# Probabilities as the stationary operand in the product with the context, in a fused gated cross-attention and expert block

## The chip, the cores and the metric

The program runs on one core of a Trainium2 chip. The time is device time in microseconds for one execution, and the figure that counts is the median of the runs. A core has a matrix engine (PE; its weight loads are shown apart, as PEld), a vector engine (DVE), an activation engine (ACT), a general engine (POOL) and a queue that issues transfers (SP). Each works through its own instructions in order; they meet at semaphores. A matmul holds one operand in the array (stationary, loaded by a LDWEIGHTS) and streams the other past it (moving); its result goes to PSUM, which has 8 banks of 512 fp32 columns.

## The reference

There are 16 batches, each with 100 query tokens of width 128 and a context of 1444 rows of width 96; cross-attention has 16 heads of width 64. What matters here, cut down:

```python
q = heads(layernorm(x) @ w_q);  k = heads(context @ w_k);  v = heads(context @ w_v)
attn = softmax(q @ k.T / 8, axis=-1)            # per head: 100 x 1444
x = x + tanh(g_xattn) * (merge(attn @ v) @ w_o + b_o)
# then self-attention over the 100 tokens (16 heads of width 8),
# a router over 8 experts (two picked), the experts and a shared expert
x = x + tanh(g_ffn) * ffn(layernorm(x))
```

## The kernel before

The weights of keys and queries are folded into one matrix per head (`Mh`), those of values and output into another (`Nh`). So the kernel never makes keys or values: scores are the context times `qk` (96 x 1600, the 16 heads' 100 queries side by side), and the product of probabilities and values is (probabilities times context) times `Nh`.

The cross-attention of one batch goes in 24 steps, numbered 0 to 23. The first twelve belong to heads 0 to 7 (half 0, 800 query columns), the others to heads 8 to 15 (half 1). Within a half each step takes one chunk of up to 128 context rows (the twelfth has 36). In step i PE first computes the scores of chunk i (`score_unit`, six matmuls of 400 columns, in fp16 parts hi*hi, hi*lo and lo*hi). ACT takes two exponentials of them (`probs`), one fp32 into `p32` and one fp16 into `p_hi`. DVE, or POOL in the even steps from 6 to 20, subtracts the two into `p_lo` (`probs_rest`). PE then multiplies the probabilities of step i-2 with the context (`pv_unit`, L747): stationary is the chunk of context (`c_hi` or `c_lo`, 128 x 128, whose column 96 is all ones so that the sum of the probabilities comes along), moving are 400 columns of probabilities, six matmuls in all. The result, context dimension by query, gathers in two PSUM banks (`ACCB`) over twelve steps. ACT copies it to `acc_sb` (`acc_evac`, at steps 13 and 1) and the next half starts in the same banks.

Everything else of a batch is cut into small units, which a plan (`plan`) places into the 24 steps: `t` and `q` transpose the next batch's context and make its `qk`; 39 `p` units compute a bound for the scores of the next batch, each one matmul of 512 or 420 columns (L813) whose row maximum DVE takes (L1247); `y` units multiply `acc_sb` with `Nh` (L840), three heads to a unit with the sum in a 129th column, DVE divides by that sum (L1265, L1269) and POOL adds the heads one by one onto `x1` (`add_heads`, L566); `ln`, `xf` and `f0` to `f13` are the self-attention; `rs` and `h2` the norm before the router. Half 1 of a batch is finished in the next batch (`y1`), half 0 in its own (`y0`).

The units that use PE share two PSUM banks in turn (`AUXB`). A unit waits until the unit two before it in this order has been read out of its bank. DVE does that reading for nearly all units; for `f6` to `f9` ACT does it (`by_act`, L999), and ACT does it after the two exponentials of its step. Within a step PE works in this order: scores, the first third of the step's units, the two hi*hi matmuls of the product with the context, the second third, the other four matmuls, the last third. A list of n units is cut at n//3 and 2n//3. The other engines keep the same order of units. The plan's `p` units go where the plan's own figures for DVE's load (`LOAD`) leave room, in steps 3 to 20.

In steps 1 to 6 this gives, with the thirds parted by a bar: step 1 `t2 | q0 | q1`; step 2 `q2 | q3 | y1,0`; step 3 `y1,1 | p0 | p1`; step 4 `y1,2 | p2 | p3`; step 5 `p4 | p5 | p6`; step 6 `ln | p7 | p8`. Then step 8 `xf | f0 | p13`; step 9 ` | f1 | p14`; step 10 ` | f2 | p15`; step 14 `f8 | p21 | p22 p23`; step 15 `y0,0 | f9 p24 | p25 p26`; step 16 `y0,1 | f10 | p27`.

After the last batch a list (`LAST`) mixes the remaining units of that batch with the first pieces of the experts; the rest of the experts follows.

## Time and profile before

| | us |
|---|---|
| median of 3 runs (lowest, highest) | 1574.19 (1571.65, 1574.80) |
| span of the profiled execution | 1570.3 |
| median over that span | 3.9 |
| sixth batch (batch 5), steps 0 to 23, from 490.6 to 571.9 | 81.3 |
| start of batch 0 / of batch 15 / end of batch 15's steps | 70.2 / 1328.4 / 1405.0 |

The profiled execution's own time isn't listed apart from its span; the 3.9 us between the span and the median of the runs stand for what lies around it. In a row of the timeline the columns are the start in us from the span's start, the time from the first start to the last end, the engine, the line, the operation with its tiles and shapes (partitions x elements; before a matmul's shape stands rows*columns of the stationary operand), and xcount, how many were merged. A matmul's shown duration holds the time to drain the array, so matmuls that follow each other overlap in it, and their pace is the distance of their starts. An fp32 matmul has two records.

### The profile page before, as it was taken

How to read it: one execution, taken by the hardware profiler on the slowest of the kernel's cores; microseconds unless marked ns; L12 is line 12 of the kernel's file. 1: busy time of each engine (PE TensorE's matmuls, PEld its weight loads, DVE VectorE, ACT ScalarE, POOL GpSimd, SP SyncE). 2: the span in 40 equal slices, each digit the busy share in tenths (PEclk: the TensorE clock that was granted, in tenths of full speed). 3: DMA queues.
4: the chain of work that ended last, by engine and by line, in shares of the span. 5: the costliest groups of instructions: out<-in, count | busy, mean ns of one | idle time of the engine just before them, and what ended most of it. 6: DMA issues, size and time to landing. Idle time of an engine off the chain costs nothing.

```text
span 1570.3 us, 29033 instructions
## 1 busy us (share of the span) xinstructions
PE 1432.2 (91%) x8968; PEld 849.7 (54%) x8968; DVE 1085.7 (69%) x1948; ACT 832.3 (53%) x1236; POOL 561.2 (36%) x705
## 2 busy tenths in 40 slices
...
DMA packets 14994, 18.08 MB, mean 12 GB/s; under 512 B 3046, under 2 KB 12490, under 8 KB 14858
## 3 DMA queue, kind: packets, MB, share of 16 engines
...
## 4 chain that ended last, share of the span: by engine, by line
PE 59%; DVE 17%; issue 9%; ACT 6%; POOL 5%; DMA 1%; DVEq 1%; POOLq 0%; ACTq 0%; SPq 0%
PE psum L747 13%; PE psum L728 7%; PE psum L813 6%; PE psum L732 6%; PE psum L730 6%; DVE mx L1247 4%; PE psum L840 4%; PE psum L760 3%; PE psum L862 3%; ACT p_hi L952 3%; PE psum L853 3%; PE psum L773 2%; DVE p_lo L431 2%; DVE kbd L1276 2%; POOL p_lo L431 2%
## 5 line engine op out<-in xcount | busy, mean ns | idle before, releaser
L951 ACT ACTIVATE p<-psum 128x800 f32<-128x800 f32 (+1 forms) x384 | 321.3, 837 | 564.1 <-PE psum L732 558.2
L1247 DVE TENSOR_REDUCE mx<-psum 128x1 f32<-128x512 f32 (+3 forms) x624 | 387.2, 652 | 63.5 <-PE psum L813 58.5
L431 POOL TENSOR_TENSOR p_lo<-p,p_hi 128x800 f16<-128x800 f32 x128 | 236.3, 1847 | 472.9 <-ACT p_hi L952 461.2
L952 ACT ACTIVATE p_hi<-psum 128x800 f16<-128x800 f32 (+1 forms) x384 | 318.8, 830 | 0.0
L431 DVE TENSOR_TENSOR p_lo<-p,p_hi 128x800 f16<-128x800 f32 (+1 forms) x256 | 269.2, 1051 | 54.5 <-ACT p_hi L952 25.5
L813 PE MATMUL psum<-cT_hi,qk_hi 96*128 96x512 f16 (+3 forms) x624 | 236.2, 389 | 47.2 <-DVE mx L1247 15.0
L747 PE MATMUL psum<-p_hi,c_hi 128*128 128x400 f16 (+1 forms) x768 | 197.4, 338 | 21.3 <-POOL p_lo L431 14.7
L728 PE MATMUL psum<-qk_hi,cT_hi 97*128 97x400 f16 (+1 forms) x768 | 198.3, 340 | 11.7 <-ACT p_hi L952 5.5
L730 PE MATMUL psum<-qk_lo,cT_hi 96*128 96x400 f16 (+1 forms) x768 | 198.0, 339 | 0.0
L732 PE MATMUL psum<-qk_hi,cT_lo 96*128 96x400 f16 (+1 forms) x768 | 197.3, 339 | 0.0
L747 PE MATMUL psum<-p_lo,c_hi 128*128 128x400 f16 (+1 forms) x768 | 195.9, 336 | 0.0
L747 PE MATMUL psum<-p_hi,c_lo 128*128 128x400 f16 (+1 forms) x768 | 195.0, 336 | 0.0
L813 PEld LDWEIGHTS psum<-cT_hi,qk_hi 96*128 96x128 f16 (+1 forms) x624 | 61.2, 98 | 175.5 <-DVE mx L1247 71.9
L566 POOL TENSOR_TENSOR y_sum<-y_sum,y_sb 100x128 f32<-100x128 f32 x192 | 107.9, 562 | 55.3 <-DVE y_sb L1269 32.9
L556 POOL TENSOR_TENSOR c_lo<-ctx_nat,c_hi 128x1056 f16<-128x1056 f32 (+1 forms) x32 | 40.1, 1273 | 234.9 <-ACT c_hi L940 234.9
L747 PEld LDWEIGHTS psum<-p_hi,c_hi 128*128 128x128 f16 (+1 forms) x768 | 70.6, 100 | 80.2 <-issue 26.4
L730 PEld LDWEIGHTS psum<-qk_lo,cT_hi 96*128 96x128 f16 (+1 forms) x768 | 76.0, 99 | 58.5 <-issue 4.2
L732 PEld LDWEIGHTS psum<-qk_hi,cT_lo 96*128 96x128 f16 (+1 forms) x768 | 75.2, 98 | 59.4 <-issue 5.1
L747 PEld LDWEIGHTS psum<-p_hi,c_lo 128*128 128x128 f16 (+1 forms) x768 | 74.8, 97 | 57.5 <-issue 2.7
L728 PEld LDWEIGHTS psum<-qk_hi,cT_hi 97*128 97x128 f16 (+1 forms) x768 | 68.7, 99 | 63.6 <-issue 30.8
L747 PEld LDWEIGHTS psum<-p_lo,c_hi 128*128 128x128 f16 (+1 forms) x768 | 72.3, 101 | 50.6 <-issue 13.2
L621 POOL TENSOR_TENSOR p_lo<-p,p_hi 128x400 f16<-128x400 f32 x72 | 67.7, 945 | 73.6 <-ACT p_hi L966 73.3
...
## 6 DMA issues: line engine op xcount, KB each, us to landing
...
```

The costliest lines, as they stand in the source:

```text
L431: engine.tensor_tensor(p_lo[0:m, i % 3, :, :], p32[0:m, i % 3, :, :], p_hi[0:m, i % 3, :, :], ALU.subtract).then_inc(lo_made(b, i)[0], 1)
L566: g.tensor_tensor(to, x, y, ALU.add).then_inc(y_add, 1)
L621: g.tensor_tensor(hid_lo[:, n % HS, :], hidden[:, n % 3, :], hid_hi[:, n % HS, :], ALU.subtract).then_inc(hid_lo_out, 1)
L728: mm(outs[k], cT_hi[parity][:, cols], qk_hi[parity][:, qs[k]], start=True, stop=False)
L730: mm(outs[k], cT_hi[parity][0:C, cols], qk_lo[parity][:, qs[k]], start=False, stop=False)
L732: t = mm(outs[k], cT_lo[parity][:, cols], qk_hi[parity][0:C, qs[k]], start=False, stop=True)
L747: t = mm(outs[k], w[parity][0:m, j, :], p[0:m, i % 3, k, :], start=(j == 0 and w is c_hi and p is p_hi), stop=(j == CH - 1 and w is c_lo))
L813: t = mm(bank[0:r, 0:w], qk_hi[parity][0:C, rt * P:rt * P + r], cT_hi[parity][0:C, part * MW:part * MW + w], start=True, stop=True)
L840: t = mm(bank[0:S, k * YW:(k + 1) * YW], acc_sb[half][:, h // 4, (h % 4) * S:(h % 4 + 1) * S], Nh[:, half * HALF + h, :], start=True, stop ...
L951: a(p32[0:m, i % 3, :, :], src, ACT.Exp, scale=DH ** -0.5)
L952: a(p_hi[0:m, i % 3, :, :], src, ACT.Exp, scale=DH ** -0.5).then_inc(probs_hi, 1)
L1247: v.tensor_reduce(mx[0:r, rt, part:part + 1], bank[0:r, 0:w], AX.X, ALU.max)\
```

## The change

The probabilities become the stationary operand. A step's 768 (half 0) or 832 (half 1) probability columns, padded to 896, are cut into 6 or 7 tiles of 128, and for each tile three matmuls stream the 96 or 97 columns of the context chunk: 18 or 21 matmuls for six. The split of the 1600 query columns is no longer at a head (768 and 832 for 800 and 800). The result stands with queries on partitions, so the sum of the probabilities is a column. ACT reads it in two instructions, POOL raises the sums to the power -1 and multiplies by them (`normalise`), and new units `a0` and `a1` (two each) turn the result back with 13 PE transposes per batch; ACT reads them into `aT` (`turned_out`), after the step's exponentials. The product with `Nh` then gathers all heads of a half in one bank: one unit `y0` (7 heads) and one `y1` (9 heads) of 128 columns a head, which DVE adds to `x1` in one instruction. The eight adds of a half on POOL, and DVE's reciprocals and multiplications of `y`, go away. The plan becomes, for the steps that differ: 2 ` | q2 | q3`; 3 `p0 | p1 | p2`; 4 `a1,0 | p3 | p4`; 5 `a1,1 | p5 | p6`; 6 `y1 | p7 | p8`; 7 `ln | p9 | p10 p11`; 8 ` | p12 | p13`; 9 `xf | f0 p14 | p15 p16`; 10 ` | | f1`; 11 `f2 | p17 | p18`; 12 ` | f3 | p19`; 13 `f4 | f6 | p20 p21`; 14 `f5 | f7 | p22`; 15 `f8 | p23 p24 | p25 p26`; 16 `f9 | p27 | p28`; 17 `a0,0 | f10 p29 | p30 p31`; 18 `a0,1 | p32 | p33`; 19 `y0 | f11 p34 | p35 p36`; 20 `f12 | p37 | p38`. The square of the layer norm and the output share other tiles' memory. The core of the diff:

```diff
-    YB = [(0, 1, 2), (3, 4, 5), (6, 7)]
-    YW = D + 1
+    TILES, PER_BANK = (6, 7), (3, 4)
+    WIDE = (6 * P // 2, (ROWS - 6 * P) // 2)
+    ROW0 = (0, 6 * P)
+    PW = 2 * WIDE[1]
+    Y_HEADS = (range(0, 7), range(7, H))
...
-    for n, i in enumerate((2, 3, 4)):
-        plan[i].append(("y1", n))
-    for n, i in enumerate((15, 16, 17)):
-        plan[i].append(("y0", n))
-    plan[6].append(("ln", 0))
-    plan[8].append(("xf", 0))
-    for n, i in enumerate((8, 9, 10, 11, 12, 13, 12, 13, 14, 15, 16, 18, 19, 23)):
+    for n, i in enumerate((4, 5)):
+        plan[i].append(("a1", n))
+    plan[6].append(("y1", 0))
+    for n, i in enumerate((17, 18)):
+        plan[i].append(("a0", n))
+    plan[19].append(("y0", 0))
+    plan[7].append(("ln", 0))
+    plan[9].append(("xf", 0))
+    for n, i in enumerate((9, 10, 11, 12, 13, 14, 13, 14, 15, 16, 17, 19, 20, 23)):
         plan[i].append(("f", n))
-    plan[20].append(("rs", 0))
+    plan[21].append(("rs", 0))
     plan[22].append(("h2", 0))
 
-    CTX_AT, Y0_AT = 3, 18
+    CTX_AT, NORM1_AT, ACC0_AT = 3, 7, 15
...
-        p_hi = sb("p_hi", [P, 3, 2, GW], F16)
-        p_lo = sb("p_lo", [P, 3, 2, GW], F16)
-        acc_sb = [sb(f"acc_sb{g}", [C + 1, 2, GW]) for g in range(2)]
+        p32 = sb("p32", [P, 3, PW])
+        p_hi = sb("p_hi", [P, 3, TILES[1] * P], F16)
+        p_lo = sb("p_lo", [P, 3, TILES[1] * P], F16)
+        acc_sb = [sb(f"acc_sb{g}", [P, TILES[g], C + 1]) for g in range(2)]
+        acc_rc = sb("acc_rc", [P, TILES[1]])
+        minus_one = sb("minus_one", [P, TILES[1]])
+        aT = sb("aT", [C, sum(TILES) * P])
...
-            def add_heads(b, half, n, free_of):
-
-                done = b * 2 * HALF + half * HALF
-
-                def add(n, to, x, y):
-                    if n:
-                        wait_apart(pool, y_add, done + n)
-                    g.tensor_tensor(to, x, y, ALU.add).then_inc(y_add, 1)
-
-                y = y_sb[:, (half * len(YB) + n) % 2, :, :]
-                pool.wait_ge(aux_free, free_of((f"y{half}", n)))
-                for k, h in enumerate(YB[n]):
-                    if h:
-                        add(h - 1, y_sum[:, :], y[:, 0, :] if h == 1 else y_sum[:, :], y[:, k, :])
-                if n == len(YB) - 1:
-                    xb = x1[:, bat(b), :].squeeze(1)
-                    add(HALF - 1, xb, xb, y_sum[:, :])
+            def normalise(b, half):
+
+                n, t = TILES[half], acc_sb[half]
+                pool.wait_ge(acc_out, b * 2 + (half + 1))
+                g.tensor_tensor(acc_rc[:, 0:n], t[:, :, C], minus_one[:, 0:n], ALU.pow).then_inc(acc_rcp, 1)
+                wait_apart(pool, acc_rcp, b * 2 + (half + 1))
+                g.tensor_tensor(t[:, :, 0:C], t[:, :, 0:C], acc_rc[:, 0:n].unsqueeze(2).broadcast_to([P, n, C]),
+                                ALU.mult).then_inc(acc_norm, 1)
...
+                    if i == NORM1_AT and kind != "first":
+                        norm_1(b - 1)
+                    if i == ACC0_AT:
+                        normalise(b, 0)
...
-                outs = [psum[:, ACCB + k, 0:GW] for k in range(2)]
-                for w, p in ((c_hi, p_hi), (c_hi, p_lo), (c_lo, p_hi)):
-                    for k in range(2):
-                        t = mm(outs[k], w[parity][0:m, j, :], p[0:m, i % 3, k, :],
-                               start=(j == 0 and w is c_hi and p is p_hi), stop=(j == CH - 1 and w is c_lo))
-                    if w is c_hi and p is p_hi:
+                half = i // CH
+                for p, c, wide in ((p_hi, c_hi, C + 1), (p_hi, c_lo, C), (p_lo, c_hi, C + 1)):
+                    for n in range(TILES[half]):
+                        bank, k = divmod(n, PER_BANK[half])
+                        t = mm(psum[:, ACCB + bank, k * (C + 1):k * (C + 1) + wide],
+                               p[0:m, i % 3, n * P:(n + 1) * P], c[parity][0:m, j, 0:wide],
+                               start=(j == 0 and k == 0 and c is c_hi and p is p_hi),
+                               stop=(j == CH - 1 and p is p_lo), skip_group_check=True)
+                    if c is c_hi and p is p_hi:
                         between()
...
-                elif kind in ("y0", "y1"):
+                elif kind in ("a0", "a1"):
                     half = int(kind[1])
                     if n == 0:
-                        pe.wait_ge(acc_out, b * 2 + (half + 1))
-                    for k, h in enumerate(YB[n]):
-                        t = mm(bank[0:S, k * YW:(k + 1) * YW], acc_sb[half][:, h // 4, (h % 4) * S:(h % 4 + 1) * S],
-                               Nh[:, half * HALF + h, :], start=True, stop=True)
+                        pe.wait_ge(acc_norm, b * 2 + (half + 1))
+                    for k in range(n * PER_BANK[half], min(TILES[half], (n + 1) * PER_BANK[half])):
+                        at = (k - n * PER_BANK[half]) * P
+                        t = tr(bank[0:C, at:at + P], acc_sb[half][:, k, 0:C], ident[:, :])
+                elif kind in ("y0", "y1"):
+                    heads = Y_HEADS[int(kind[1])]
+                    pe.wait_ge(*released(("a" + kind[1], 1), b))
+                    for h in heads:
+                        t = mm(bank[0:S, 0:D], aT[:, h * S:(h + 1) * S], Nh[:, h, :],
+                               start=(h == heads[0]), stop=(h == heads[-1]))
...
-                a(acc_sb[half][:, :, :], psum[0:C + 1, ACCB:ACCB + 2, 0:GW], ACT.Copy).then_inc(acc_out, 1)
+                for bank in range(2):
+                    t0, t1 = bank * PER_BANK[half], min(TILES[half], (bank + 1) * PER_BANK[half])
+                    ins = a(acc_sb[half][:, t0:t1, :], psum[:, ACCB + bank, 0:(t1 - t0) * (C + 1)].rearrange(
+                        "p (k c) -> p k c", c=C + 1), ACT.Copy)
+                ins.then_inc(acc_out, 1)
+
+            def turned_out(seq, par, unit, out_of, first):
+
+                half, n = int(unit[0][1]), unit[1]
+                act.wait_ge(aux_full, seq + 1)
+                if half == 0 and not first:
+                    act.wait_ge(aux_free, out_of(("y1", 0)))
+                t0, t1 = n * PER_BANK[half], min(TILES[half], (n + 1) * PER_BANK[half])
+                at = ROW0[half] + t0 * P
+                a(aT[:, at:at + (t1 - t0) * P], psum[0:C, AUXB + par, 0:(t1 - t0) * P], ACT.Copy).then_inc(at_out, 1)
...
-                    half = int(kind[1])
-                    nh = len(YB[n])
-                    heads = bank[0:S, 0:nh * YW].rearrange("p (k w) -> p k w", w=YW)
-                    at = half * len(YB) + n
+                    xb = x1[:, bat(b), :].squeeze(1)
                     dve.wait_ge(aux_free, free)
-                    v.reciprocal(y_rc[:, 0:nh], heads[:, :, D]).then_inc(y_rcp, 1)
-                    if not (isinstance(b, int) and b == 0 and at < 2):
-                        dve.wait_ge(y_add, b * 2 * HALF + (Y_READ[at - 2] - 2 * HALF * (at < 2)))
-                    dve.wait_ge(y_rcp, b * 2 * len(YB) + (at + 1))
-                    tt(y_sb[:, at % 2, 0:nh, :], heads[:, :, 0:D],
-                       y_rc[:, 0:nh].unsqueeze(2).broadcast_to([S, nh, D]), ALU.mult).then_inc(aux_free, 1)
+                    tt(xb, bank[0:S, 0:D], xb, ALU.add).then_inc(aux_free, 1)
```

## Rows read from the trace of the kernel before

**Rows 1.** The page: span, and busy time by engine.

```profile
span 1570.3 us, 29033 instructions
...
PE 1432.2 (91%) x8968; PEld 849.7 (54%) x8968; DVE 1085.7 (69%) x1948; ACT 832.3 (53%) x1236; POOL 561.2 (36%) x705
```

**Rows 2.** The chain of waits that ended last: shares of the span by engine.

```profile
PE 59%; DVE 17%; issue 9%; ACT 6%; POOL 5%; DMA 1%; DVEq 1%; POOLq 0%; ACTq 0%; SPq 0%
```

**Rows 3.** Windows: length, PE, PEld, DVE, ACT, POOL busy (x), PEclk, DMA, GB/s.

```profile
490.60:514.96 24.36, 23.11 (x154) 14.74 (x154) 16.41 (x29) 15.30 (x24) 7.42 (x11) 1.00 0.08 24
514.96:531.52 16.56, 15.28 (x81) 7.73 (x80) 13.91 (x23) 9.04 (x13) 7.85 (x9) 1.00 0.01 1
531.52:565.26 33.74, 32.37 (x202) 19.25 (x200) 23.17 (x43) 17.74 (x26) 11.65 (x12) 1.00 0.00 1
565.26:571.92 6.66, 6.66 (x39) 3.48 (x39) 4.26 (x8) 4.05 (x7) 2.83 (x5) 1.00 0.01 0
1328.40:1405.00 76.60, 68.53 (x401) 40.82 (x399) 54.65 (x93) 42.43 (x60) 34.94 (x35) 0.91 0.00 1
```

**Rows 4.** Groups by line: count, busy us, mean ns, idle before.

```profile
L747 PE MATMUL psum<-p_hi,c_hi 128*128 128x400 f16 (+1 forms) x768 | 197.4, 338 | 21.3 <-POOL p_lo L431 14.7
```

**Rows 5.** Timeline, PE: start us, us from first start to last end, line, xcount.

```profile
493.07 0.60 PE L802 MATMUL psum<-ident,ctx_nat 128*96 128x128 f32 x4
...
711.68 0.83 PE L840 MATMUL psum<-Nh,acc_sb 97*100 97x129 f32 x6
...
716.85 2.91 PE L862 MATMUL psum<-v,pT 100*100 100x9 f32 x32
```

**Rows 6.** Groups by form, weight loads (PEld).

```profile
L747 PEld LDWEIGHTS psum<-p_hi,c_lo 128*128 128x128 f16 x704 | 68.7, 98 | 52.9 <-issue 2.7
...
L773 PEld LDWEIGHTS psum<-wd_hi,p_hi 128*100 128x100 f16 x288 | 35.9, 125 | 17.6 <-POOL p_lo L621 9.8 <-DVE x L1162 2.1 <-issue 1.8
```

**Rows 7.** Timeline, PE, experts: first and last of twelve in a row, and next.

```profile
1483.80 0.22 PE L773 MATMUL psum<-wd_hi,p_hi 128*100 128x128 f16 x1
...
1484.42 0.22 PE L773 MATMUL psum<-wd_hi,p_lo 128*100 128x128 f16 x1
...
1484.47 0.33 PE L760 MATMUL psum<-h_hi,wg_hi 128*128 128x400 f16 x1
```

**Rows 8.** Timeline, step 14 of batch 7, PE and ACT.

```profile
707.91 0.51 PE L858 MATMUL psum<-ident,ex 100*100 100x100 f32 x4
...
708.25 0.84 ACT L951 ACTIVATE p<-psum 128x800 f32<-128x800 f32 x1 [0.87 <-PE psum L732]
...
708.82 0.50 PE L747 MATMUL psum<-p_lo,c_hi 128*128 128x400 f16 x2
...
709.16 0.50 PE L747 MATMUL psum<-p_hi,c_lo 128*128 128x400 f16 x2
...
709.70 0.51 ACT L999 ACTIVATE pT<-psum 100x400 f32<-100x400 f32 x1
...
710.26 0.57 PE L813 MATMUL psum<-cT_hi,qk_hi 96*128 96x512 f16 x2 [0.60 <-ACT pT L999]
```

**Rows 9.** Groups by form on DVE and POOL.

```profile
L1181 DVE TENSOR_SCALAR xf<-x,aggr,ps 100x128 f32 x14 | 14.2, 1012 | 0.0
...
L1269 DVE TENSOR_TENSOR y_sb<-psum,y_rc 100x384 f32<-100x384 f32 x64 | 35.6, 557 | 2.7
...
L1247 DVE TENSOR_REDUCE mx<-psum 128x1 f32<-128x512 f32 x384 | 257.3, 684 | 56.9 <-PE psum L813 55.7
...
L1276 DVE TENSOR_TENSOR kbd<-psum,head_mask 128x1600 f32<-128x1600 f32 x16 | 29.0, 1813 | 0.0
...
L566 POOL TENSOR_TENSOR y_sum<-y_sum,y_sb 100x128 f32<-100x128 f32 x192 | 107.9, 562 | 55.3 <-DVE y_sb L1269 32.9 <-POOL y_sum L566 0.4
...
L589 POOL TENSOR_TENSOR ps<-ps,minus_half 100x1 f32<-100x1 f32 x16 | 17.1, 1070 | 2.3 <-POOL ps L588 1.1
```

**Rows 10.** Timeline: the first unit after the last batch.

```profile
1410.98 0.88 PE L840 MATMUL psum<-Nh,acc_sb 97*100 97x129 f32 x6 [1.02 <-ACT acc_sb L957]
```

More of the change, by code:

```diff
@@ L145, in by_act @@
     def by_act(u):
-        return u[0] == "f" and 6 <= u[1] < 10
+        return u[0] in ("a0", "a1") or u[0] == "f" and 6 <= u[1] < 10
     def numbered(units):
@@ L168, in aux_base @@
     def aux_base(b, kind):
-        fixed = {"prep": (0, 0), "first": (AT_FIRST, AT_FIRST), "end": (END, END - 4 * (B - 2) - 4)}
-        return fixed.get(kind) or ((b - 1) * A + AT_LOOP, (b - 1) * (A - 4) + AT_LOOP)
+        fixed = {"prep": (0, 0), "first": (AT_FIRST, AT_FIRST), "end": (END, END - 2 - 8 * (B - 2) - 8)}
+        return fixed.get(kind) or ((b - 1) * A + AT_LOOP, (b - 1) * (A - 8) + AT_LOOP - 2)
     ODD = {"prep": 0, "first": AT_FIRST % 2, "odd": AT_LOOP % 2, "even": (AT_LOOP + A) % 2,
@@ L187, in flamingo_kernel @@
     NPS = len(P_STEPS)
-    SET_POOL = ["-1/2", "zero ident", "ident", "zero ident16", "ident16", "lnr0", "Nh right", "Nh below",
-                "Nh corner", "ones cT0", "pad c_hi0", "ones c_hi0", "pad c_lo0", "ones cT1", "pad c_hi1",
+    SET_POOL = ["-1/2", "zero ident", "ident", "zero ident16", "ident16", "lnr0", "minus one",
+                "pad p_hi", "pad p_lo", "ones cT0", "pad c_hi0", "ones c_hi0", "pad c_lo0", "ones cT1", "pad c_hi1",
                 "ones c_hi1", "pad c_lo1", "mx", "ones v9", "ones mask", "mask above", "head_mask",
@@ L359, in run_aux, with released @@
                     lambda other: base[1] + at[other][1] + 1,
-                    (pt_out, batch_of(last, b) * 4 + (last[1] - 5)) if last and by_act(last)
+                    released(last, 0 if kind == "prep" else batch_of(last, b)) if last and by_act(last)
                     else (aux_free, base[1] + last_free))
+        def released(unit, b):
+            kind, n = unit
+            return (pt_out, b * 4 + (n - 5)) if kind == "f" else (at_out, b * 4 + (n + 1 + 2 * (kind == "a1")))
         def cut(q, n):
@@ L418, in flamingo_kernel @@
         comb = xlnT[0:S, 3 * B * E:3 * B * E + B * (E + 1)].rearrange("p (b e) -> p b e", e=E + 1)
-        silu = p32[:, :, 0, :]
-        hidden = p32[:, :, 1, :]
-        hid_hi = p_hi[:, :, :, :].rearrange("p a k w -> p (a k) w")
-        hid_lo = p_lo[:, :, :, :].rearrange("p a k w -> p (a k) w")
+        silu = p32[:, :, 0:GW]
+        hidden = p32[:, :, GW:2 * GW]
+        hid_hi, hid_lo = (t[:, :, :].rearrange("p a (k w) -> p (a k) w", k=2)[:, :, 0:GW] for t in (p_hi, p_lo))
         def probs_rest(eng, engine, b, i):
-            m = kc(i % CH)[1]
+            m, w = kc(i % CH)[1], 2 * WIDE[i // CH]
             eng.wait_ge(probs_hi, b * UNITS + (i + 1))
@@ L430, in probs_rest @@
                 eng.wait_ge(pv, b * UNITS + (i - 2))
[L431 removed]
+            engine.tensor_tensor(p_lo[0:m, i % 3, 0:w], p32[0:m, i % 3, 0:w], p_hi[0:m, i % 3, 0:w],
                                  ALU.subtract).then_inc(lo_made(b, i)[0], 1)
         Mh_r = Mh[:, :, :].rearrange("p (a r) c -> p r a c", r=2)
[L435 removed]
+        Nh_r = Nh[:, :, :].rearrange("p (a r) c -> p r a c", r=2)
         wd_flat = wd[:, :, :, :].rearrange("p e a d -> p e (a d)")
@@ L536, in _ @@
             token_rstd(0)
-            step("Nh right", g.memset(Nh[:, :, D:YW], 0.0))
-            step("Nh below", g.memset(Nh[C:C + 1, :, 0:D], 0.0))
-            step("Nh corner", g.memset(Nh[C:C + 1, :, D:YW], 1.0))
+            step("minus one", g.memset(minus_one[:, :], -1.0))
+            step("pad p_hi", g.memset(p_hi[:, :, PW:], 1.0))
+            step("pad p_lo", g.memset(p_lo[:, :, PW:], 0.0))
             for q in range(2):
@@ L626, in body @@
                     token_rstd(1)
+                if kind != "first":
+                    normalise(b - 1, 1)
                 if kind != "last":
```

82 lines of the change are left out of this document (31 added, 51 removed).

## The prediction

> **What bounds the kernel now.** I read the busy times first [rows 1]: PE 91%, no other engine above 69%. The chain of waits gives PE 59%, DVE 17% and little to ACT and POOL [rows 2]. So PE's own stream comes first, and what stops it is mostly a PSUM bank that DVE or ACT hasn't read out. The windows of one batch in its four blocks of steps (0 to 6, 7 to 11, 12 to 20, 21 to 23) show where each engine stands [rows 3]. This batch has the clock at 1.00 throughout. In steps 7 to 11 DVE is busy 13.91 of 16.56 us, nearly as much as PE; in 21 to 23 PE is never idle. A busy PE hides short stalls, since a shown matmul includes its drain: the change must be worked out from starts, not from PE's 91%.
>
> **The product itself.** Two matmuls of 400 columns start 0.34 us apart, 0.17 each [rows 8]. Twelve fp16 matmuls of 128 columns, each with a stationary tile of its own, take 1484.47 - 1483.80 = 0.67 us, 56 ns each [rows 7]. The line through both is 0.42 ns a column, so 97 columns give 43 ns, if nothing but the columns sets the pace. A batch has 144 matmuls now (24 steps of 6; 768 of each of the three kinds are 16 batches of 48 [rows 4]): 24.5 us. After it there are 12 x 18 + 12 x 21 = 468 at 43 ns: 20.1 us. That removes 4.4 us of array time; a step of half 0 gets 0.25 us shorter, one of half 1 0.12.
>
> No row shows a 97-column matmul in fp16. Bounds: 43 ns below, 56 ns above (the nearest row; the pace of a pair of load and matmul is proven there). At 56 ns the product takes 26.2 us, 1.7 more than now. I take 43: the shown weight load of 128 columns is 98 ns, shorter than the 125 ns of 100 columns [rows 6], and the 125 ns one already runs behind matmuls 56 ns apart [rows 7], so loads overlap, and the 128-column kind has the more room.
>
> One rule of the skill speaks against the whole change. The Trainium skill (TensorE: Matmul & The Clock Gate, LDWEIGHTS) puts a weight load at its columns over 1.2 GHz, which is 107 ns for 128, whatever the rows; 468 of them in series would be 50 us a batch. The trace disagrees where it can be seen: 56 ns for a load of 100 columns with its matmul. The same page (Fast Weight Load) says that full 128-column loads of types other than fp32 take a faster path, and there the trace agrees: 98 against 125 ns.
>
> **The turning back.** 13 transposes a batch. Four of them are 0.60 us to the last end, a drain of 0.17 included (0.22 shown for a matmul at a pace of 0.056 [rows 7]), so 0.11 each [rows 5]: +1.4 us. `y` costs 0.11 a record before ((0.83 - 0.17)/6 [rows 5]), 32 records a batch, and the same 32 after: 3.5 us, nothing saved. Array time in all: -4.4 + 1.4 = -3.0 us a batch. On DVE six multiplications of some 0.5 and six reciprocals go, two adds of about 0.3 come: -3.5 us. On POOL 16 adds of about 0.56 [rows 9] go; two powers and two multiplications come. A power took 1.07 on one column [rows 9]; with seven columns between that and seven times it, and I take 1.1, since one instruction's fixed part weighs most in so short a row; a multiplication of 576 or 672 elements lies above the 0.56 of 128 elements and below five times it, 2.8: taken at 1.5. POOL has the time: `normalise` of half 1 may start at the end of step 1 and is wanted in step 4, that of half 0 has steps 15 and 16. ACT gets four copies of about 0.5 (`pT`'s 400 columns take 0.51 [rows 8]): +2.1 us.
>
> **What the units then wait for.** The stretch in rows 8 gives the rule for a unit that ACT reads out. The scores end at 707.91 (the unit's first matmul), ACT's exponentials start at 708.25, the copy at 709.70, and the bank is released at 710.26: S + 2.35 us, S being the end of the scores. PE had finished its own work by 709.16 + 0.34 = 709.50 and stood 0.76 us. The faster PE gets between S and that bank's next use, the longer it stands: in such a step the saved array time is given back. DVE's release is its queue plus 0.68 for a `p` [rows 9].
>
> I follow the new plan with that, step by step. PE's array time in a step after the change is 0.98 + 0.77 in half 0 (six score matmuls of 384 columns, 18 of 97), 1.06 + 0.90 in half 1, 0.98 + 0.90 in steps 0 and 1, and the units: 0.2 a `p` (512 or 420 columns on the line above), 0.11 a transpose of 128 columns, 0.34 for `f6` to `f9` (0.51 less the drain [rows 8]), and for fp32 matmuls 0.85 ns a column and record (0.11 for `y`'s 129): 0.22 a head of `y`, 0.69 a `q`, 0.68 for `f2` to `f5`, 0.64 for `f1`, 2.75 for `f10` [rows 5]. Summed by blocks of steps: 21.1, 12.2, 30.0 and 6.1.
>
> **Steps 0 to 6** (24.36 now). Step 1 keeps its wait of about 0.9 for `t2`'s bank. Step 4 is `a1,0 | p3 | p4`: p4 needs a1,0's bank. ACT is also late here (it has the context's conversion and two `q` copies before), so it is released at S + 2.6; PE would come at S + 0.44 + 0.26 + 0.22 + 0.51 = 1.4: 1.3 with p3's wait. Step 5, `a1,1 | p5 | p6`: 2.35 - 1.35 = 1.0. Some 0.7 more at `q3` and p0. Sum 25.0, +0.6; the three `y1` units with their stalls in steps 2 to 4 are gone in this figure.
>
> **Steps 7 to 11** (16.56 now). PE has 12.2 of its own, but DVE nearly 14. Step 9: `f0` needs two DVE instructions of `xf` (1.01 [rows 9] and one that I take at 0.35), and they stand behind `p_lo` and two row maxima of the steps before: it waits 1.5, and 0.2 more go at the following bank. Step 10 holds `f1` alone and in the last third, and step 11 has `f2` in the first: between them lie the score matmuls only (1.0), where DVE needs 1.81 for `f1`'s `kbd` [rows 9] and two copies of about a hundred columns before it (taken at 0.25 each, below the 0.56 of 384 columns): 1.6, and 0.5 for p18. Sum 16.0, -0.5.
>
> **Steps 12 to 20** (33.74 now). Step 13: f6's copy comes after the exponential of f4, released at S + 3.1, wanted at 2.2: with p20 1.2. Step 15, `f8 | p23 p24 | p25 p26`: p24 wants f8's bank already at S + 0.34 + 0.30 + 0.22 = 0.86, so 1.5, and 0.3 for p26. Step 16, `f9 | p27 | p28`: 2.35 - 1.46 = 0.9. Step 17: `f10`, 2.75 us of narrow matmuls [rows 5], covers a0,0. Step 18, `a0,1 | p32 | p33`: 0.9. Steps 14, 19 and 20 together 0.6. Sum 35.5, +1.8.
>
> **Steps 21 to 23** (6.66 now): PE-bound, 3 x 0.12 less, 0.2 back at ACT: 6.5, -0.2.
>
> A batch: 0.6 - 0.5 + 1.8 - 0.2 = +1.7 us; times 14 (batches 1 to 14) +24. Batch 0 is set by the layer norms on DVE: 0. Batch 15 has no `p`, `t` and `q` units (PE 68.5 of 76.60 us [rows 3]); array time is saved in part: -2. At the end `y1,0` waited 1.02 us for ACT [rows 10]; now POOL's power and multiplication come between (about 3 us) and all experts queue behind `a1,0`: +3. Span: 1570.3 + 24 - 2 + 3 = 1595.3; with the 3.9 us around it, which is the distance to the median 1574.19, 1599.
>
> **The rivals.** (1) *PE's saved time is kept.* It decides if the banks that ACT reads hold PE for less than 0.3 us a step in the six steps named. For it: PE 91%, and POOL's adds no longer hold up `p_lo` (14.7 us of PE's idle time in all [rows 4]). If stalls stay as they are, 16 x 3.0 = 48 less: 1526; if half is given back, 1550. Against it: the four `a` units and p24. (2) *Pace of 56 ns.* Then 0.24 to 0.28 us a step; in the six steps with a copy on ACT the wait absorbs it, in the other 18 not: 4.6 us a batch, 15.5 batches, +71: 1670. In between, at 48 ns, 1627. (3) *A wash.* The six waits on ACT come to 5.0 us a batch instead of my 6.8 (1.3 + 1.0 + 1.2 + 1.5 + 0.9 + 0.9), because ACT starts its copies earlier: 1.7 x 14 = 24 less, so 1575. (4) *Loads in series*, 98 ns each as shown [rows 6]: 468 x 98 ns = 45.9 us, +21.4 a batch, 330 over all: about 1900. The skill's 1.2 GHz rule above is this case with a dearer load. The rows of the experts leave it almost nothing.
>
> **How the numbers follow.** Forecast 0.50, within 1582 to 1618 by itself; (1) 0.27, (2) 0.12, (3) 0.09, (4) 0.02. Bounds 1550 to 1645 leave out the far ends of (1), (2) and all of (4). About 0.2% (3 us) is what a measurement of this kernel can tell from no change. Faster: 0.27 and a third of (3), 0.30. Same: 0.06. Slower: 0.64.
>
> **What would show it.** Starts of the new matmuls 43 ns apart: else (2). PE idle before `p` matmuls, released by ACT's copy to `aT` or `pT`, in steps 4, 5, 13, 15, 16 and 18, about 1 us each: if missing, the forecast fails towards (1). DVE between `f1` and `f2`: 2.3 us in which PE stands 1.6. No PE wait for POOL's `p_lo`. ACT 2.1 us a batch more, DVE 3.5 and POOL 2 to 4 less. One wait of about 4 us for POOL after the last batch. The 1.2 GHz stretches that some batches have are taken as unchanged; more of them would be a cause that I left out.

## The result, and the profile after

The kernel after takes 1664.37 us (median of 4 runs, 1661.67 to 1669.96), the one before 1573.99 on the same chip: ratio 1.0586, 95% interval 1.0552 to 1.0620. The sign was forecast, the size was not: +90 us where +25 were worked out.

The page after, the lines that answer to [rows 1, 2, 4] (span and busy time; the shares of the chain; product matmuls and their weight loads):

```profile
span 1659.9 us, 38914 instructions
...
PE 1409.7 (85%) x14360; PEld 1007.9 (61%) x14360; DVE 1071.2 (65%) x1788; ACT 857.8 (52%) x1332; POOL 539.6 (33%) x513
...
PE 62%; DVE 15%; issue 11%; ACT 9%; POOL 1%; DMA 1%; DVEq 1%; ACTq 0%; SPq 0%; POOLq 0%
...
L734 PEld LDWEIGHTS psum<-c_hi,p_hi 128*128 128x128 f16 (+1 forms) x2496 | 148.1, 99 | 72.4 <-issue 37.4
L734 PE MATMUL psum<-c_hi,p_hi 128*128 128x97 f16 (+1 forms) x2496 | 176.4, 210 | 10.2 <-ACT acc_sb L955 5.8
```

PE is busy 22 us less in a span 90 us longer: it stands more. POOL no longer shows up as the releaser of the product, as forecast.

The four windows of batch 5, the even batch behind it, and batch 15 (columns as in [rows 3]):

```profile
513.43:541.09 27.66, 24.15 (x253) 18.55 (x254) 16.24 (x22) 16.43 (x27) 7.74 (x5) 0.94 0.07 22
541.09:558.90 17.81, 13.70 (x141) 8.98 (x139) 15.16 (x24) 7.80 (x11) 6.75 (x10) 1.00 0.00 1
558.90:595.73 36.83, 32.92 (x335) 23.44 (x334) 21.75 (x37) 19.38 (x30) 10.30 (x6) 1.00 0.01 2
595.73:602.21 6.48, 6.48 (x84) 4.65 (x84) 4.81 (x10) 4.02 (x6) 3.75 (x5) 1.00 0.01 1
602.21:694.45 92.24, 77.66 (x811) 55.78 (x809) 58.59 (x92) 49.24 (x75) 28.54 (x25) 0.98 0.03 8
1414.68:1486.20 71.52, 64.07 (x723) 48.90 (x720) 51.38 (x83) 43.58 (x67) 28.71 (x22) 0.93 0.01 2
```

The blocks were forecast at 25.0, 16.0, 35.5 and 6.5. By the starts of the first score matmul of each batch, batches 1 to 14 took 1170.9 us before and take 1262.9 now (+92.0; 83.6 and 90.2 each), set-up -2.2, batch 0 -3.5, batch 15 -5.1, all behind it +8.3.

Where PE stands in batch 5 (timeline of PE, the rows with idle time, which stands in brackets with its releaser; steps 4, 5, 7, 9, 11, 13, 15, 16 and 18):

```profile
531.79 0.64 PE L830 MATMUL psum<-ident,acc_sb 128*96 128x128 f32 x4 [1.75 <-DVE mx L1259]
536.74 0.39 PE L802 MATMUL psum<-cT_hi,qk_hi 96*128 96x512 f16 x1 [0.82 <-ACT aT L967]
...
544.93 0.35 PE L802 MATMUL psum<-cT_hi,qk_hi 96*128 96x420 f16 x1 [0.74 <-DVE mx L1259]
550.09 0.30 PE L839 MATMUL psum<-ident,hn 100*128 100x100 f32 x1 [1.38 <-DVE hn L1195]
556.41 0.92 PE L848 MATMUL psum<-kbd,qT 128*100 128x400 f32 x2 [1.20 <-DVE kbd L1279]
...
565.87 0.39 PE L802 MATMUL psum<-cT_hi,qk_hi 96*128 96x512 f16 x1 [0.56 <-ACT pT L1011]
573.03 0.39 PE L802 MATMUL psum<-cT_hi,qk_hi 96*128 96x512 f16 x1 [1.41 <-ACT pT L1011]
577.85 0.39 PE L802 MATMUL psum<-cT_hi,qk_hi 96*128 96x512 f16 x1 [0.76 <-ACT pT L1011]
587.64 0.39 PE L802 MATMUL psum<-cT_hi,qk_hi 96*128 96x512 f16 x1 [0.80 <-ACT aT L967]
```

The waits for ACT and for `f0` and `f2` are those forecast. The first and third rows are not, and their causes are visible. DVE and POOL at the first, taken here from batch 7, where the same wait of 1.75 us stands (duration behind the start):

```profile
709.02 3.23 POOL L564 TENSOR_TENSOR c_lo<-ctx_nat,c_hi 128x1056 f16<-128x1056 f32 x2 [0.63 <-ACT c_hi L935]
709.50 2.53 DVE L439 TENSOR_TENSOR p_lo<-p,p_hi 128x768 f16<-128x768 f32 x1
711.95 1.18 DVE L1259 TENSOR_REDUCE mx<-psum 128x1 f32<-128x512 f32 x2
712.76 0.64 PE L830 MATMUL psum<-ident,acc_sb 128*96 128x128 f32 x4 [1.75 <-DVE mx L1259]
713.05 0.94 DVE L439 TENSOR_TENSOR p_lo<-p,p_hi 128x768 f16<-128x768 f32 x1
```

The same subtraction takes DVE 0.94 us alone and 2.53 beside POOL's. The third row's cause lies in step 6 of batch 5:

```profile
537.94 2.13 PE L835 MATMUL psum<-Nh,aT 96*100 96x128 f32 x18
539.95 1.64 POOL L439 TENSOR_TENSOR p_lo<-p,p_hi 128x768 f16<-128x768 f32 x1 [8.66 <-ACT p_hi L948]
540.33 0.29 DVE L1273 TENSOR_TENSOR x<-psum,x 100x128 f32 x1 [2.47 <-PE psum L835]
540.53 1.86 DVE L439 TENSOR_TENSOR p_lo<-p,p_hi 128x768 f16<-128x768 f32 x1
```

`y1` is first in DVE's order of the step, and its eighteen matmul records (nine heads of two) end late: DVE stands 2.47 us with `p_lo` queued behind the add, and then meets POOL's. DVE's record ends 0.8 us after POOL's (539.95 + 1.64 to 540.53 + 1.86), nearly the 0.94 of the instruction alone: it ran when POOL's was done. That is what the Trainium skill (SBUF — State Buffer, SBUF: two separate sides) says of a DVE instruction with two SBUF inputs and a POOL one that reads SBUF: the one that starts later is blocked until the first has ended. This trace agrees.

Last, the loop's jump. PE's sequencer at the loop's line, seven times (duration min/median/max in ns), after and then before:

```profile
L331 PEldq COMPARE_BRANCH  x7: 83/3487/3843, 328.5 to 1414.1; - x7
```

```profile
L327 PEldq COMPARE_BRANCH  x7: 76/3558/3777, 320.3 to 1326.1; - x7
```

The jump costs 3.5 us in both. What differs is PE's work already handed over. The end of batch 4, after and before:

```profile
507.04 0.47 PE L734 MATMUL psum<-c_hi,p_hi 128*128 128x97 f16 x7
507.34 0.46 PE L734 MATMUL psum<-c_lo,p_hi 128*128 128x96 f16 x7
...
510.12 0.27 PE L867 MATMUL psum<-ident,hn 100*128 100x100 f32 x1
513.43 0.82 PE L714 MATMUL psum<-qk_hi,cT_hi 97*128 97x384 f16 x2 [3.04 <-issue]
```

```profile
488.61 0.50 PE L747 MATMUL psum<-p_hi,c_lo 128*128 128x400 f16 x2
488.95 0.25 PE L872 MATMUL psum<-ident,hn 100*128 100x100 f32 x1
490.59 0.51 PE L728 MATMUL psum<-qk_hi,cT_hi 97*128 97x400 f16 x2 [1.39 <-ACT p_hi L952]
```

By starts, PE stands 3.31 us against 1.64 (3.24 to 3.67 and 1.47 to 1.88 over the six edges). The branch starts at 509.67 and 486.77; 11 matmuls start behind it in 0.45 us, where 13 of 0.17 us lasted 2.18 before. After, a stretch at 1.2 GHz follows each edge (PEclk 0.94 in the first window). The first two rows also give the product's pace: 0.30/7 = 43 ns.

### The profile page after: what moved, and what is told of

Read it like the earlier page. It is cut to its first block, busy times and chain, and to the rows that moved or that the text cites. A ratio compares the mean times of both kernels' runs of the same rounds, so it can differ in the third digit from the quotient of the medians.

```text
span 1659.9 us, 38914 instructions
## 1 busy us (share of the span) xinstructions
PE 1409.7 (85%) x14360; PEld 1007.9 (61%) x14360; DVE 1071.2 (65%) x1788; ACT 857.8 (52%) x1332; POOL 539.6 (33%) x513
## 4 chain that ended last, share of the span: by engine, by line
PE 62%; DVE 15%; issue 11%; ACT 9%; POOL 1%; DMA 1%; DVEq 1%; ACTq 0%; SPq 0%; POOLq 0%
PE psum L734 12%; PE psum L802 8%; PE psum L714 7%; PE psum L718 6%; PE psum L716 6%; ACT p_hi L948 4%; DVE mx L1259 4%; PE psum L749 4%; PE psum L835 3%; PE psum L794 3%; PE psum L857 3%; PE psum L848 3%; PE psum L762 2%; DVE kbd L1279 2%; DVE hn L1195 1%
## 5 line engine op out<-in xcount | busy, mean ns | idle before, releaser
L947 ACT ACTIVATE p<-psum 128x768 f32<-128x768 f32 (+3 forms) x384 | 320.9, 836 | 601.8 <-PE psum L718 511.6
L439 POOL TENSOR_TENSOR p_lo<-p,p_hi 128x832 f16<-128x832 f32 (+1 forms) x128 | 234.1, 1829 | 677.3 <-ACT p_hi L948 593.3
L948 ACT ACTIVATE p_hi<-psum 128x768 f16<-128x768 f32 (+3 forms) x384 | 318.5, 829 | 0.0
L439 DVE TENSOR_TENSOR p_lo<-p,p_hi 128x768 f16<-128x768 f32 (+3 forms) x256 | 286.4, 1119 | 31.2 <-issue 18.1
L714 PE MATMUL psum<-qk_hi,cT_hi 97*128 97x384 f16 (+3 forms) x768 | 199.4, 341 | 21.9 <-issue 18.9
L716 PE MATMUL psum<-qk_lo,cT_hi 96*128 96x384 f16 (+3 forms) x768 | 197.4, 338 | 0.0
L718 PE MATMUL psum<-qk_hi,cT_lo 96*128 96x384 f16 (+3 forms) x768 | 195.8, 337 | 0.0
L734 PE MATMUL psum<-c_hi,p_hi 128*128 128x97 f16 (+1 forms) x2496 | 176.4, 210 | 10.2 <-ACT acc_sb L955 5.8
L734 PE MATMUL psum<-c_hi,p_lo 128*128 128x97 f16 (+1 forms) x2496 | 174.1, 209 | 0.0
L734 PE MATMUL psum<-c_lo,p_hi 128*128 128x96 f16 (+1 forms) x2496 | 173.5, 209 | 0.0
L620 POOL TENSOR_TENSOR p_lo<-p,p_hi 128x400 f16<-128x400 f32 x72 | 67.5, 943 | 86.0 <-ACT p_hi L976 85.7
```

What stands on the lines that cost most here:

```text
L439: engine.tensor_tensor(p_lo[0:m, i % 3, 0:w], p32[0:m, i % 3, 0:w], p_hi[0:m, i % 3, 0:w], ALU.subtract).then_inc(lo_made(b, i)[0], 1)
L620: g.tensor_tensor(hid_lo[:, n % HS, :], hidden[:, n % 3, :], hid_hi[:, n % HS, :], ALU.subtract).then_inc(hid_lo_out, 1)
L714: mm(outs[k], cT_hi[parity][:, cols], qk_hi[parity][:, qs[k]], start=True, stop=False)
L716: mm(outs[k], cT_hi[parity][0:C, cols], qk_lo[parity][:, qs[k]], start=False, stop=False)
L718: t = mm(outs[k], cT_lo[parity][:, cols], qk_hi[parity][0:C, qs[k]], start=False, stop=True)
L734: t = mm(psum[:, ACCB + bank, k * (C + 1):k * (C + 1) + wide], p[0:m, i % 3, n * P:(n + 1) * P], c[parity][0:m, j, 0:wide], start=(j == 0 ...
```

## The experiments

Ratios are to the kernel before on the same chip. "Stretches" are pieces of 3.41 us with the granted clock at 1.2 GHz in batches 1 to 14, which begin in the step named: 11 before, 14 after. Times of steps are means over batches 1 to 14, stretches included.

**e1_act_last**

```
+    for i in plan:
+        plan[i].sort(key=lambda u: u[0] in ("a0", "a1") or u[0] == "f" and 6 <= u[1] < 10)
```

> Each step's units are the same, but the ones whose bank ACT reads (a0, a1, f6 to f9) come last in their step. Theory A (a bank that ACT holds until its two exponentials are through stops PE): the idle time of PE before `p` matmuls put down to ACT, 62 us in the changed kernel, goes below 15, steps 5, 13, 15, 16 and 18 get some 0.8 us shorter each, and the time falls from 1664 to about 1612. Rival B (these waits only cover a DVE that is as late): the same waits come back under DVE's name and the time stays above 1650.

1629.83 us, 1.0354 (1.0323 to 1.0385). Steps 5, 13, 15, 16 and 18 fell from 3.53, 4.43, 4.82, 3.68 and 3.78 to 2.86, 4.16, 3.76, 2.75 and 3.26 us; step 17 rose from 6.18 to 7.56, and there were 33 stretches, 20 of them at step 17. The waits for ACT before `p` matmuls went, as theory A says, and the time fell 35 us of the 52 that it gave; the 19 stretches more are the likeliest place of the rest, which isn't shown apart.

**e2_y1_last**

```
+    plan[6].sort(key=lambda u: u[0] == "y1")
```

> In step 6 the unit y1 comes after p7 and p8. Theory A: in the changed kernel DVE, which goes in order, waits 2.5 us for the 18 long matmuls of y1 while p_lo of step 5 stands behind them, and step 7 pays with 1.67 us of standing PE; with y1 last step 7 falls from 4.03 to about 2.6 us and the time from 1664 to about 1643. Rival B (step 7 stands for the norm and DVE's load): less than 5 us of change, 1660 to 1668.

1666.16, 1.0579 (1.0541 to 1.0618): no gain, though step 7 fell from 4.03 to 2.59 and the `p_lo` that DVE makes in step 6 from 1.93 to 0.95. The step did what theory A says, the time what B says. Stretches: 34.

**e3_little_clo**

```
                 for r, js in CTX_PARTS:
+                    if not (isinstance(b, int) and b == 0):
+                        js = slice(js.stop - 1, js.stop)
```

> Left out: from the second batch on POOL computes the low part of the context for one chunk only instead of eleven, so that its instruction at step 3 lasts some 0.3 us, not 2.2. Theory A (DVE and POOL can't both work on operands in SBUF at that moment, and DVE's p_lo of step 2, 2.53 us long in the changed kernel instead of 0.94, is held by POOL): p_lo takes 0.95 in step 3, step 4 falls from 5.22 to about 3.9 us, and the time from 1664 to about 1645. Rival B (step 4 stands for ACT's copy of a1,0 or for POOL's normalise): DVE's p_lo gets shorter but step 4 stays above 4.8 us and the time above 1658.

1649.08, 1.0498 (1.0463 to 1.0534). This kernel leaves out most of the context's low part. `p_lo` beside it 2.53 to 1.03 us, step 4 from 5.22 to 3.58; six of the 14 stretches of the kernel after begin in step 4, so by the medians it is 4.59 to 3.58. The collision is the cause of step 4's stall. Stretches: 22.

**e4_unrolled** (SP's loop likewise; the same edit is e5 on the kernel before)

```
-            with eng.Fori(0, (B - 2) // 2) as r:
+            for r in range((B - 2) // 2):
```

> The loop over pairs of batches is written out, nothing else. Theory A (the jump back costs PE 3.2 us at each of six edges, and 3.4 us at half clock after it, which is why even batches take 92.1 us and odd ones 88.8): all batches take about 88.8 us and the time is about 1644. Rival B (PE runs short of instructions whatever the loop, since it has 60% more of them): stretches without a matmul of about 3 us stay, elsewhere, and the time stays above 1655 or rises.

1608.98, 1.0237 (1.0214 to 1.0261): 55 us of the 90 went, far more than theory A's 20, and B is refuted. Stretches: 8.

**e5_before_unrolled**

> The kernel before with the loop over pairs of batches (and that of the queue on SP) written out. What it gains is what the loop's edges cost the kernel before; the kernel after lost 53.7 us to the same edit (1664.4 less about 1610 us). Theory A: the edges cost the kernel before less, since PE stands 1.5 to 1.9 us at each of its six edges against 3.2 to 3.7 after, and no stretch at 1.2 GHz follows them: 10 us for the standing, 5 to 15 for what comes behind it, so 1545 to 1560 us; then some 30 to 40 of the 90 us between the kernels are the edges. Theory B: the edges cost both alike: 1520 us, and nothing of the 90 us is theirs.

1556.73, 0.9901 (0.9871 to 0.9932), so 16 us: the loop explains 39 of the 90. Stretches: 17. Theory A by its size, but at some 1.4 us a stretch about 16 of the 39 are the clock: the stretches fell by six in one kernel and rose by six in the other. Written out, batches at 2.4 GHz throughout can be compared, first after (e4, batch 5) and then before (e5, batch 9):

```profile
497.27:523.08 25.81, 22.77 (x256) 17.42 (x254) 16.52 (x23) 17.16 (x28) 7.88 (x5) 1.00 0.08 23
523.08:540.44 17.36, 13.69 (x140) 8.78 (x139) 14.81 (x24) 7.79 (x11) 6.36 (x10) 1.00 0.00 1
540.44:576.47 36.03, 32.84 (x335) 23.06 (x333) 21.92 (x37) 19.38 (x30) 10.49 (x7) 1.00 0.01 2
576.47:582.96 6.49, 6.49 (x85) 4.66 (x85) 4.59 (x10) 4.16 (x6) 3.59 (x5) 1.00 0.02 3
```

```profile
818.04:842.23 24.19, 23.08 (x156) 14.68 (x154) 16.81 (x30) 15.92 (x25) 8.23 (x11) 1.00 0.08 24
842.23:858.21 15.98, 15.30 (x81) 7.54 (x80) 13.44 (x23) 8.91 (x13) 7.56 (x10) 1.00 0.00 0
858.21:892.30 34.09, 32.39 (x202) 18.92 (x200) 25.04 (x43) 17.78 (x26) 11.01 (x13) 1.00 0.00 1
892.30:898.97 6.67, 6.67 (x40) 3.49 (x39) 4.03 (x8) 4.14 (x6) 2.81 (x5) 1.00 0.01 0
```

85.7 against 80.9 us: the change costs 4.8 us a batch where neither clock nor loop has a part.

**e6_no_turn** (both `a` and `y` units and `normalise` taken out)

```
-    for n, i in enumerate((4, 5)):
-        plan[i].append(("a1", n))
-    plan[6].append(("y1", 0))
```

> The kernel after without the four units that turn the sums back, without both y units and without POOL's power and multiplication: only the new product and its evacuation are left of the change (x1 lacks the attention over the context). Theory A: the product itself is no loss; what is lost hangs on the turning back. PE has 4.9 us a batch less to do (13 transposes 1.4, y 3.5), ACT's four copies and the waits for them (24.0 us by the profile) go, and DVE's wait for the first y unit as well: 7 to 8 us a batch less, 1540 to 1565 us. Theory B: the narrow matmuls of the product with their evacuation in pieces set the time, and the turning only fills gaps: not under 1610 us.

1566.69, 0.9955 (0.9924 to 0.9987), against 1664: theory A, but for 2 us, and with 40 stretches. The narrow product with its evacuation doesn't set the time. More isn't shown: the run also leaves out the `y` units, 3.5 us of PE's work a batch that the kernel before does, and no run takes those out of the kernel before.

**e7_combo**

```
-    CTX_AT, NORM1_AT, ACC0_AT = 3, 7, 15
+    CTX_AT, NORM1_AT, ACC0_AT = 17, 7, 15
```

with the edits of e1, e2 and e4, and `ctx_lo` issued behind step 16's `p_lo`.

> The kernel after with four edits at once: within each step the units whose bank ACT reads out come last, y1 comes last in its step, the split of the next context runs at step 17 instead of 3 (so that POOL's subtraction no longer lies beside DVE's at steps 2 and 3), and the loop is written out. Theory A: the stalls named in steps 4, 5, 7, 13, 15 and 16 and the edges are separate costs that add up, about 1609 less 30 to 50: 1560 to 1580 us. Theory B: what is saved in those steps is given back in step 17 and by stretches at 1.2 GHz, as in the three single edits: 1595 to 1610 us.

1530.27, 0.9717 (0.9667 to 0.9767): faster than both kernels, and than either theory allowed. Stretches: 10, all at step 17. Two of its batches, without and with one:

```profile
555.67:635.64 79.97, 75.36 (x812) 53.48 (x810) 55.28 (x91) 49.21 (x74) 27.73 (x25) 1.00 0.03 9
635.64:716.97 81.33, 76.72 (x811) 54.48 (x809) 55.31 (x91) 49.20 (x74) 27.73 (x25) 0.98 0.03 8
```

Same work: 1.4 us for this stretch.

**e8_before_combo** (the same on the kernel before, without `y1`)

> The kernel before with those of the same edits that it can take: units read out by ACT last in their step, the split of the next context at step 17, the loop written out. Theory A: the order of units is part of what the change disturbed and the kernel before has little to gain from it: within 10 us of the kernel before written out alone. Theory B: the order is worth the same in both, and 20 us or more are gained against it.

1598.17, 1.0150 (1.0100 to 1.0201): 41 us slower than e5. Both theories missed. Steps 13 and 14 rose from 4.96 and 3.94 to 6.20 and 5.03, with 30 stretches, 19 at step 13; the 13 stretches more than in e5 are about half of the 41 us. What suits one kernel's order spoils the other's.

**e9_edge_cover**

```
                     run_aux(aux, three, b, kind, parity)
+                    if kind == "even" and i == UNITS - 1:
+                        score_unit(b, parity, i)
```

> The kernel after with one thing moved: in the last step of the loop's body (step 23 of an even batch) the six score matmuls, 0.17 us each, are issued behind the product's 63 instead of ahead of them. In both kernels PE's sequencer takes 3.4 to 3.9 us for the jump back; what differs is how much work PE has been handed when it jumps: 13 matmuls that last 2.2 us before, 11 that last 0.45 us after. Theory A: that cover is the cause of the longer stand at the edge; with six of 0.17 and five of 0.04 us behind the branch it is 1.2 us, so PE stands 2.4 to 2.8 us at an edge instead of 3.2 to 3.7, and the kernel is 5 to 8 us faster than after, 1656 to 1659 us. Theory B: it is something else, such as the amount of instructions to be fetched: PE stands 3.2 to 3.7 us as before the edit, and the time stays at 1664 or rises.

1662.61, 1.0598 (1.0563 to 1.0633): no gain. The first score behind the jump:

```profile
510.59 0.51 PE L718 MATMUL psum<-qk_hi,cT_lo 96*36 96x416 f16 x2
513.78 0.82 PE L714 MATMUL psum<-qk_hi,cT_hi 97*128 97x384 f16 x2 [2.67 <-ACT p_hi L951]
```

Six matmuls now start behind the branch, over 0.93 us instead of 0.45, and PE stands 2.68 to 3.26 us by starts, 2.93 on the mean for 3.42. The 0.49 us are what the longer cover gives: theory A's mechanism, but 3 us in all, and here are 19 stretches for 14, which can take that back.

**e10_u_ctx17, e11_u_y1_last, e12_u_act_last**: each edit of the combination alone, on e4.

> On the kernel after with its loop written out (1609 us), one edit: the split of the next context is made at step 17 instead of 3, and POOL's subtraction for it behind its p_lo of step 16. Theory A: DVE's p_lo(2) falls from 2.5 us to about 1 us, PE's stall in step 4 goes (4.43 to about 3.2 us), 14 to 20 us in all: 1589 to 1595 us, if the collision isn't only moved to step 17. Theory B: it is only moved there, or the stall behind ACT takes its place: 1604 us or more.

> On the kernel after with its loop written out (1609 us), one edit: y1 comes last of the units of step 6. In the looped kernel step 7 got 1.44 us shorter by it and the total no shorter, with 1.2 GHz stretches up from 47.8 to 116 us. Theory A: the order is worth 1 us a batch, 14 us, and the clock took it back: written out, with fewer stretches, 1592 to 1598 us. Theory B: what is gained in step 7 is lost to the clock here too: 1605 us or more, with over 80 us at 1.2 GHz.

> On the kernel after with its loop written out (1609 us), one edit: the units whose bank ACT reads out (a0, a1, f6 to f9) come last of their step's units. Theory A: the waits for ACT in steps 5, 13, 15, 16 and 18 go, 2.8 us a batch less 0.5 that step 17 takes back: 30 to 42 us, 1567 to 1579 us; together with the other two edits that accounts for the 79 us by which all three at once were faster. Theory B: the edits help only together (each alone leaves another unit late): under 20 us, 1590 us or more.

Against 1608.98: 1598.09 (ratio 1.0190, 1.0136 to 1.0245), 1607.19 (1.0236, 1.0206 to 1.0267) and 1582.17 (1.0079, 1.0050 to 1.0109). None came within theory A's time, and e11's is theory B's. The steps did what A said: step 4 from 4.43 to 3.45 in e10 (its `p_lo` 2.45 to 0.95), step 7 from 3.59 to 2.66 in e11; the times did so in part, since the stretches rose from 8 to 14, 18 and 23. A batch of e12 with two stretches and one with none:

```profile
491.47:576.80 85.33, 78.65 (x812) 55.47 (x810) 57.43 (x91) 49.23 (x74) 28.37 (x25) 0.96 0.03 8
576.80:659.09 82.29, 75.62 (x811) 53.41 (x809) 57.40 (x91) 49.22 (x74) 28.36 (x25) 1.00 0.03 8
```

1.5 us each. Over all runs a batch with one stretch is 0.5 to 1.7 us longer than one of the same kernel with none, so the 1.5 is rough. Taking it for each from batches 1 to 14:

| kernel | batches 1-14, us | stretches | without them | gain |
|---|---|---|---|---|
| e4 | 1209.2 | 8 | 1197.2 | |
| e10 | 1202.8 | 14 | 1181.8 | 15.4 |
| e11 | 1208.0 | 18 | 1181.0 | 16.2 |
| e12 | 1186.4 | 23 | 1151.9 | 45.3 |
| e7, all three | 1134.4 | 10 | 1119.4 | 77.8 |

15.4 + 16.2 + 45.3 = 76.9: the edits add up, and what looked like an effect of having them together (40 us singly, 79 together) is mostly the clock. Batches without a stretch say so without the 1.5: they take 85.7, 84.7, 84.8, 82.3 and 80.0 us in the table's order, gains of 1.0, 0.9 and 3.4 singly, some 5.2 added up, and 5.7 together.

**e13_combo_loop** (e7 with its loops)

> The combination of three edits (ACT's units last, y1 last, split of the next context at step 17), 1530 us with its loop written out, here with the loop kept. Theory A: the six jumps and what follows them cost the changed kernel 50 to 55 us in any order of units: 1578 to 1586 us, slower than the kernel before with its loop (1573), so that the sign of the change hangs on the loop. Theory B: the jumps cost that much only where DVE and ACT were late already, and little in the combination: under 1560 us.

1570.22, 0.9978 (0.9949 to 1.0007): no change against before, between the theories. The loop costs 40 us here, with 23 stretches for e7's 10.

**e14_f10_mid** and **e15_f10_spread**, on e7

```
+    plan[17].insert(2, plan[17].pop(0))
```

```
+            def some(n):
+                for _ in range(min(n, len(later))):
+                    out_, left, right = later.pop(0)
+                    t = mm(out_, left, right, start=True, stop=True)
+                    if not later:
+                        t.then_inc(aux_full, 1)
```

with `some(1)` behind each matmul of the product.

> The combination written out (1530 us) with f10's place within step 17 moved from the first third to the middle, behind two p units. It is the base of the next run. Theory A (the clock falls behind f10's narrow matmuls, wherever they stand): time within 5 us of 1530, some ten stretches at 1.2 GHz in batches 1 to 14, now beginning 0.5 us or so later in the step. Theory B: f10 was waiting for f9's copy on ACT, and the later place saves that, 5 us or more: 1525 us or less.

> As the run before, and f10's 32 matmul records of 9 columns no longer stand in a block of 2.7 us but are issued two by two between the 128-wide loads and 97-column matmuls of the product. PE's work is the same. Theory A: the block of narrow matmuls is what precedes the fall to 1.2 GHz in step 17; spread out, the ten stretches there shrink to under three, step 17 gets 0.5 to 1 us shorter and the kernel 5 to 12 us faster, 1518 to 1525 us. Theory B: the fall comes from PE standing in steps 15 to 17 or from something else: as many stretches, the same time within 3 us.

1531.90 (0.9733, 0.9677 to 0.9789) and 1542.50 (0.9800, 0.9744 to 0.9856). In e14 A held, with 11 stretches; e15 missed both ways: 14 stretches, one in each batch, and slower. `f10` ends 0.35 us later, and `a0,0` waits for its bank. The stretches come without a block of narrow matmuls too.

**e16_f02_last**, on e7

```
+    for i in (9, 11):
+        plan[i].sort(key=lambda u: u in (("f", 0), ("f", 2)))
```

> The combination written out (1530 us), with f0 last in step 9 and f2 last in step 11, behind the p units. I had put the stalls of steps 9 and 11 down to the DVE work right ahead of these units (xf and kbd, 1.5 and 1.6 us). Theory A: the p units and the product cover them: steps 9 and 11 fall from 4.18 and 4.84 to about 3.2 and 3.6 us, and with 0.3 given back in steps 10 and 12 the kernel is 20 to 28 us faster, 1502 to 1512 us. Theory B: DVE itself is the bound of steps 9 to 13, so that what these two steps save comes back in 10, 12 and 13: within 6 us of 1530.

1514.43, 0.9627 (0.9571 to 0.9682), the fastest here, short of theory A's 1502 to 1512 us. PE's waits of e7 and then of e16 (us, times, longest):

```profile
PE psum L842 <- DVE hn L1198: 24.4, 15, 5.5
PE psum L851 <- DVE kbd L1282: 19.1, 16, 1.3
PE psum L805 <- DVE mx L1262: 10.9, 36, 1.3
```

```profile
PE psum L808 <- DVE mx L1265: 23.9, 48, 1.3
PE psum L808 <- DVE kbd L1285: 9.2, 14, 0.7
...
PE psum L845 <- DVE hn L1201: 5.5, 1, 5.5
```

Step 11 fell from 4.84 to 3.82, step 9 only from 4.18 to 4.03. The first was order; in step 9 the wait changed its name, from `hn` (1.35 us a batch) to `mx` (0.98 and 0.21), and DVE stays the bound. What an order of its own would give the kernel before wasn't tried beyond e8.

## Why the prediction was wrong

**The product.** 43 ns, as worked out [rows 7, 8], against the bound of 56 and loads in series; rival (2) came near the measured time by another way and is refuted. `y`'s 32 records kept their 0.11 us. Array time by starts fell about 2.4 us a batch, forecast 3.0, and that is what shows the product to be no loss; e6 can't, as it leaves out `y` as well.

**The turning back's waits.** Forecast 1.0, 1.2, 1.5, 0.9 and 0.9 behind ACT in steps 5, 13, 15, 16 and 18; the rows show 0.82, 0.56, 1.41, 0.76 and 0.80, each counted from the drain's end, some 0.17 less than from the start. `f0` 1.38 for 1.5, `f2` 1.20 for 1.6. PE waits for ACT for 62 us in all. POOL's powers took 1.67 us on the mean, not 1.1, without delaying a batch; behind the last batch the wait for POOL is 4.0 us, as forecast. From e5's undisturbed batch to e4's DVE is 1.5 us less busy, forecast 3.5, POOL 1.3, forecast 2 to 4, and ACT 1.7 more, forecast 2.1. A slip without weight: steps 21 to 23 were given as 6.1 of PE's own and 0.2 of wait, but entered at 6.5, which is what they take.

**The step that failed** is the sum of blocks 0 to 6 and 7 to 11, "25.0" and "16.0", and then the carrying over of "a batch: +1.7" to all fourteen. On e4's undisturbed batch the blocks are 25.8, 17.4, 36.0 and 6.5: 85.7 for 83.0, or 38 us over 14 batches. In step 4 I had only ACT's bank; DVE's `p_lo` beside POOL's `c_lo` was priced as if alone, and in step 6 I followed PE's side of `y1` only, not that DVE waits for its eighteen records with `p_lo` queued behind. They are 0.98 us (e10) and 0.93 us (e11) a batch, 27 of the 38; the other 11, about half in steps 7 to 11 and half in 12 to 20 by the blocks, weren't tried apart.

The loop and the clock carry the rest. Over an undisturbed batch the mean batch is longer by 90.2 - 85.7 = 4.5 us after, 83.6 - 81.3 = 2.3 in the profile before: 2.2 x 14 = 30 us. Of it 6 x 1.7 = 10 are PE's stand at the jumps (the same jump, less queued ahead of it) and 3 x 1.5 = 4.5, roughly, the three more stretches; the last 15 lie in many steps at 0.1 to 0.4 us each (step 7 falls from 4.03 to 3.59 written out), and their cause stays open. One candidate is in the traces: in batch 5 the sequencers of the looped kernel after run 111 register operations (ALU_OP) on PE, 96 on DVE and 64 on ACT, 3.6, 3.9 and 2.2 us of them, and e4's none. The kernel before has as many (115, 113 and 59) and loses less off the edges (81.3 against 80.9 us in e5), so it would have to be that they matter more where an engine is late already; no run tries that. The prediction had named the clock as a cause left out; the jump it had not thought of. Set-up, batch 0, batch 15 and the end give -3.5 against their forecast: 38 + 30 - 3.5 = 65, the miss.

**The rivals.** (1), saved time kept, is wrong for this order. e16 is 42 us faster than e5, near the 48 that (1) named, but that is no proof of it: part comes from the place of `f0` and `f2`, which the kernel before was never given. (3) named 5.0 us for the six waits behind ACT; 0.82 + 0.56 + 1.41 + 0.76 + 0.80 + 5 x 0.17 = 5.2 are seen in five, for which the forecast had 5.5, since step 4's came from DVE. These waits were forecast rightly; the miss lies elsewhere.

What starts a stretch stays open. Most begin where PE has stood (steps 4 and 0) or behind `f10`, and one sits in some batches of a kernel and not in others with the same steps.
